# Two orders in the second attention: ScalarE's direct heads between two copies, and TensorE's next scores in front of the fourth turn

## The reference

```python
q = proj(query, w_q, b_q)          # 16 heads of 16 features
k = proj(key, w_k, b_k)
v = proj(value, w_v, b_v)
scores = jnp.einsum('bhqd,bhkd->bhqk', q, k) / np.sqrt(D_K)
attn = jax.nn.softmax(scores, axis=-1)
out = jnp.einsum('bhqk,bhkd->bhqd', attn, v)
out = out.transpose(0, 2, 1, 3).reshape(B, S, D_MODEL)
out = jnp.einsum('bsd,ed->bse', out, w_o) + b_o
```

## Time and profile before

| what | value |
|---|---|
| median of 3 runs | 601.71 us (600.31 to 602.09) |
| the profiled execution's own time | 600.69 us |
| its span | 599.0 us |
| TensorE's mean granted clock over the span | 0.953 |
| busy share of TensorE, VectorE, ScalarE, POOL over the span | 86%, 63%, 53%, 25% |
| second attention, from the first scores to the last turns | about 296 to 400 us |

### The profile page before, as it was taken

The page is one execution under the profiler, slowest core; times in us unless marked ns, Lnnn a source line. Parts: engine busy times, 40 slices in busy tenths (PEclk is TensorE's granted clock), DMA queues, the critical chain, the costliest instruction groups (busy, mean ns, idle before and its releaser), DMA issues.

```text
span 599.0 us, 9299 instructions
## 1 busy us (share of the span) xinstructions
PE 513.8 (86%) x3283; PEld 362.7 (61%) x3283; DVE 376.5 (63%) x937; ACT 317.3 (53%) x654; POOL 152.6 (25%) x218
## 2 busy tenths in 40 slices
PE   0869999899999700899989999996799999999994
PEld 0548866644444300787657687874667776777773
DVE  6765689945489989788688699987403432143101
ACT  1527658823389969781388899984222112211220
POOL 2716525000000000000323133111234354434531
PEclk9979999999999955999999999999699999999998
DMA  7900000000000000025000001015133536353410
GB/s 227 308 4 2 1 2 1 2 0 1 0 0 0 1 1 0 1 77 205 1 1 2 21 18 37 2 37 176 28 110 120 185 119 204 116 184 119 134 44 22
DMA packets 31994, 37.58 MB, mean 63 GB/s; under 512 B 8656, under 2 KB 27728, under 8 KB 31952
## 3 DMA queue, kind: packets, MB, share of 16 engines
q1 hardware_dynamic: 28880, 29.07, 15.0%
q0 software_dynamic: 3072, 7.95, 4.6%
HBM read 30.14 MB, written 6.88 MB: 62 GB/s over the span
## 4 chain that ended last, share of the span: by engine, by line
PE 68%; DVE 16%; ACT 10%; issue 2%; DMA 2%; SPq 1%; POOLq 0%; POOL 0%; DVEq 0%
PE pA L2043 12%; PE pB L2061 9%; PE pC L1712 6%; PE pC L1751 5%; PE pA L1745 3%; PE pB L1761 3%; ACT arena L609 3%; PE pA L1667 2%; PE pC L1575 2%; PE pC L1667 2%; PE pB L1667 2%; ACT XIT L706 2%; PE pC L2054 2%; DVE am L1168 2%; PE pB L1841 2%
## 5 line engine op out<-in xcount | busy, mean ns | idle before, releaser
L487 POOL TENSOR_TENSOR arena<-KT,par 128x256 f32<-128x256 f32 x32 | 18.9, 613 | 248.3 <-DVE XIT L1242 186.4
L2043 PE MATMUL pA<-arena 128*128 128x320 f32 x256 | 74.1, 438 | 0.4 <-ACT arena L882 0.4
L894 ACT ACTIVATE arena<-pA 128x320 f32<-128x320 f32 x64 | 28.0, 437 | 71.9 <-PE pA L2043 71.2
L2061 PE MATMUL pB<-arena 128*128 128x256 f32 x256 | 59.3, 385 | 0.0
L2043 PEld LDWEIGHTS pA<-arena 128*128 128x128 f32 x256 | 47.4, 190 | 18.9 <-issue 1.1
L2061 PEld LDWEIGHTS pB<-arena 128*128 128x128 f32 x256 | 47.4, 190 | 9.4 <-issue 3.1
L1134 DVE TENSOR_REDUCE am<-arena 128x1 f32<-128x512 f32 x48 | 32.1, 681 | 23.0 <-ACT arena L646 22.9
L1712 PE MATMUL pC<-wdnT,XIT 128*128 128x256 f32 x192 | 42.9, 381 | 1.8 <-DVE XIT L1242 1.8
L1318 DVE TENSOR_REDUCE rm<-pA 128x16 f32<-128x2048 f32 x16 | 36.7, 2291 | 8.7 <-PE pA L1745 8.7
L1712 PEld LDWEIGHTS pC<-wdnT,XIT 128*128 128x128 f32 x192 | 36.0, 190 | 7.9 <-DVE XIT L1242 2.8
L523 POOL DMA_INDIRECT out<-arena,token x24 | 23.5, 978 | 55.0 <-DVE arena L1466 43.9
(11 more groups left out here) (342 smaller groups left out, 1156.5 us busy)
## 6 DMA issues: line engine op xcount, KB each, us to landing
arena<-in_L_ffn_wi SPq DMA_DIRECT2D x8, 1024.0 KB, 5.4
arena<-in_L_ffn_wo SPq DMA_DIRECT2D x8, 1024.0 KB
X<-in_x SPq DMA_DIRECT2D x4, 512.0 KB, 5.7
arena<-in_ctx SPq DMA_DIRECT2D x4, 512.0 KB, 5.9
out<-X SPq DMA_DIRECT2D x4, 512.0 KB, 2.9
token_rows<-arena SPq DMA_DIRECT2D x4, 512.0 KB, 5.5
arena<-in_L_ffn_w_up SPq DMA_DIRECT2D x1, 768.0 KB, 9.1
arena<-in_L_ffn_w_gate SPq DMA_DIRECT2D x1, 768.0 KB, 10.2
```

What stands on the lines that cost most here:

```text
L894: nc.scalar.activation(HT[:, u, f, :], ps[2 + f % 2][:, 0:ROWS], ACT.Relu).then_inc(s["h_relu"], 1)
L2043: last = mm(ps[2 + f % 2][:, 0:ROWS], WI[:, u, k, f * P:(f + 1) * P], XET[:, u, k, :], start=(k == 0), stop=(k == KD - 1))
L2061: last = mm(ps[4 + c][:, 0:D], HT[:, u, f, c * P:(c + 1) * P], WO[:, u, f, :], start=(f == 0), stop=(f == NFT - 1))
```

## The change

On ScalarE, `direct(x)` moves in front of copy 2 of row y: it now stands between copies 1 and 2. On TensorE, `scores1(x+1)` moves in front of `turn_3(y)`. Nothing is added or removed, and no wait inside a step changes.

```diff
@@ ScalarE's loop
                     q_out(3, 1)
                 if 0 <= y < NB:
                     pt_copy(y, y % 2, 1)
+                if x < NB:
+                    direct(x, x % 2)
+                if 0 <= y < NB:
                     pt_copy(y, y % 2, 2)
                 if x < NB:
-                    direct(x, x % 2)
                     exps(x, x % 2, 0)
                 if 0 <= y < NB:
                     pt_copy(y, y % 2, 3)
@@ TensorE's loop
                     a_out(a, a % 2)
                 if 0 <= o < NB:
                     o_turn(o, o % 2)
+                if x + 1 < NB:
+                    scores1(x + 1, (x + 1) % 2)
                 if 0 <= y < NB:
                     turn_3(y, y % 2)
-                if x + 1 < NB:
-                    scores1(x + 1, (x + 1) % 2)
                 if x < NB:
                     turn_0(x, x % 2)
```

## The result

The changed kernel takes 606.25 us in the median of 7 runs (604.19 to 607.03), the kernel before 601.75 (600.31 to 604.5, 7 runs). The ratio is 1.0074 with a 95% interval of 1.0058 to 1.0089: slower by 4.5 us, which the interval leaves open between about 3.5 and 5.4. The forecast was 606.2 in a range of 603.4 to 608.4, slower with a chance of 0.89.

The account below looks back on a forecast made before the run. The kernel was taken as bound by a loop of waits through TensorE and ScalarE, 5.86 us a turn; 3.1 + 0.4 + 0.2 + 0.0 + 0.8 = +4.5 us on the median 601.71 gave 606.2, range 603.4 to 608.4.

Parts of the forecast that it names:

- What bounded the kernel: Second attention, ordinary turn: a loop of waits through TensorE and ScalarE, in which scores wait for `direct`, gives 5.87 us.
- Copy 2 behind `direct`: ScalarE, ordinary turn: the step from copy 1 to `direct` loses one copy, a gain of 0.48 us.
- Scores in front of `turn_3`: TensorE, ordinary turn: `turn_3` starts 1.08 us behind the scores; for TensorE a swap that costs nothing.
- The hold of copy 3: ScalarE: copy 3 waits for `turn_3`, idle 0.65 us; `at_copy` comes 0.79 later, net +0.31 a turn.
- S: The start of a turn's scores, from which the prediction counts the times of the other steps in us.
- The other turns: Second attention: ten ordinary turns +3.1 us, turn 1 +0.4, turn 3 +0.2, turn 4 0.
- the seven steps: ScalarE in turn 1: copy 3 and the list behind it before `direct(2)`, about 0.5 us each, 3.5 without a pause.
- The end: After the last turn: copy 2 now stands in front of `exps(15, 0)`, for which `last_turn(0)` waits; +0.8 us.
- The price of the Trainium skill: ScalarE: 0.73 us for each copy or exponential; the turn would grow about 0.5, the sum to about +7.
- The clock: Rival, TensorE: pauses lower the clock to 1.2 GHz; two such turns give some 616 us; chance 0.01.
- The gain that comes through: Rival, ordinary turns: scores follow `o_turn` at once, each turn falls by 0.16; -2.1 us, 599.6; chance 0.04.
- VectorE's second loop: Rival: VectorE's room of some 0.15 us a turn runs out, each turn costs 0.2 more; +7, 608.7; chance 0.08.

Follow-up runs that it names:

- run 2: ScalarE's half of the change alone, against the kernel before: TensorE's `turn_3` back in front of the scores; 607.45 us, ratio 1.0101.
- Run 1: The changed kernel with `exps(x, 1)` moved in front of copy 3 on ScalarE; 601.43 us, ratio 0.9999 to the kernel before.
- Run 6: The kernel before with, from turn 4, both changed orders, `exps(x, 1)` in front of copy 3 and copy 0 in front of `at_copy`; 600.53 us, ratio 0.9985.
- 3: The changed kernel plus one idle 128x256 copy in front of copy 3 on ScalarE; 605.78 us, ratio 1.0067 to the kernel before.
- run 4: The changed kernel plus one idle 128x256 copy behind copy 3 on ScalarE; 609.43 us, ratio 1.0127 to the kernel before.

## Why the prediction was right, step by step

- **What bounded the kernel.** The loop that I walked in the rows of before (scores, `turn_0`, `a_turn`, `at_copy`, copy 0, `turn_1`, copies 1 and 2, `direct`) was the right one. Six further kernels moved or loaded its steps, and every ordinary turn came out within 0.01 of what was expected (5.81 for 5.82, 6.36, 6.17, 6.47, 6.65 for 6.66, 5.80 for 5.79), the 6.36 with the reserve told at run 2.
- **Copy 2 behind `direct`: 0.48 gained.** Right: 355.37 to 355.86 is 0.49 from copy 1 to `direct`, where it was 0.97.
- **Scores in front of `turn_3`.** `turn_3` started 1.08 behind the scores, as `turn_0` had. Right. That this order costs TensorE nothing by itself is borne out by runs 1 and 6, which have it and turns of 5.81 and 5.80.
- **The hold of copy 3.** Predicted S + 1.78, measured 352.74 - 350.97 = 1.77. `exps` follows at 2.27 (2.26), `at_copy` at 2.78 (2.78), copy 0 at 3.05 (3.06), `turn_1` at 3.70 (3.70), copy 1 at 4.40 (4.40), `direct` at 4.89 (4.88), the next scores at 6.17 (6.17). I had announced an idle time of 0.65 in front of copy 3; the profile counts idle time from the end of the instruction before and says 0.48, from start to start it is 0.63. The 0.35 at `turn_1` is 0.30 in the row for the same reason.
- **The cause** is shown, not only argued: taking one exponential out of the held part removes the loss of an ordinary turn (1), and the same idle copy is free in front of the hold and costs in full behind it (3, 4).
- **The other turns.** Turn 1 and what follows to the scores of row 3: +0.53 for +0.4. The missing 0.1 is the one by which the scores of row 2 were to come sooner: they come 5.68 behind scores 1 as before, now held by VectorE's subtraction. From there the seven steps took the 3.5 of the prediction (copy 3 at 311.07, `direct` at 314.57). Turn 3: +0.21 for +0.2. Turn 4: -0.14 for 0; there `direct` ends at 338.15, early enough, and the scores at 338.63 follow `o_turn` (338.11) as soon as TensorE can. The ten ordinary turns: 9 x 0.304 + 0.30 = +3.03 for +3.1. The end: 7.51 against 6.72, +0.79 for +0.8. The sum is +4.4 for +4.5; the misses are small and partly cancel.
- **The end, read more closely.** The +0.8 there is all of the lateness of `at_copy` with nothing given back: behind the last scores TensorE waits for `exps(15, 0)`, and copy 2 stands in front of that in both orders. I had the size, but my reason, that copy 2 now stands in front of `exps(15, 0)`, is no difference between the kernels. Run 1 shows the same: its `at_copy` is 0.43 later than before, and its end takes 7.15, 0.43 more.
- **The price of the Trainium skill.** By "ScalarE: Activation LUTs", Rules for kernel authors, the turn would have grown by about 0.5 (1.25 later for `at_copy`, less 0.73 for copy 2). It grew by 0.304. Copy 3 took 0.50 of ScalarE's list (352.74 to 353.24) and the exponential 0.51 (353.24 to 353.75), where the page's figures give 0.73 for each. I had misapplied them: the page gives its 0.3 us for an activation whose bias is a `[128,1]` pointer operand, and the calls of the copies and of `exps` pass no bias. The four direct heads do pass one. For their 128 columns the figures give 0.41, an estimate, and the rows show 0.38 for each (the median of 64 before).
- **The clock.** TensorE stood still for 0.30 in front of `turn_1` in every turn. The ordinary turns are all 6.17 and eight matmuls of 128 columns take 1.09 as before. The profile's page grants nine tenths or more in all slices of this stage, the higher level of 2.4 GHz, as before; read for itself, the stretch from 303 to 406 us has a granted clock of 1.00. The rule of the Trainium skill, "TensorE: Matmul & The Clock Gate", A second HAM failure mode: psum-queue depth-cycling, did not show at pauses of this size, nor at 0.60 in run 4, whose turns are all alike too and whose granted clock is 1.00 from 338 to 400 us. One reading in the prediction was too narrow: the lower level was not granted around 210 to 240 us alone, slices 2 and 28 of the kernel before show 0.7 and 0.6, both outside the second attention.

```profile
PEclk9969999999999955999999999999699999999998
```

- **The rivals.** The gain that comes through needed `at_copy` by S + 2.43. Run 1 brings it to 2.42, and there the turn does fall below that of before, to 5.81: the point from which it decides was right. But it falls by 0.05 and not by 0.16, since `direct` stays the hold: it still stands behind copy 1, and copy 1 behind `turn_1`. Run 6, where copy 0 holds nothing any more, shows the whole of this shorter loop: `turn_1` 3.33 behind the scores, copy 1 another 0.70, `direct` 0.49, the next scores 1.29, together 5.81 for a turn of 5.80. I had overlooked that second link in the rival's price. VectorE's second loop did not close; 0.19 of its room is left, where I had walked about 0.15.

## What to carry to other kernels

When two engines with fixed lists feed each other, find the loop of waits and add it up from start to start; a step that is moved forward on it is worth what it gives only if nothing else in either list is pushed onto the loop. Moving work in front of a step delays whoever waits for that step, and everything that stands behind the waiting instruction in its own list: here the late copy 3 took 0.79 a turn, where moving copy 2 gave 0.48 back. A cheap test for where such a loop runs is an idle instruction put on either side of the suspected wait. Here, shorter than the wait, it was free on one side and cost its full slot on the other.

## What the runs showed that I had not expected

- Within each of the eight traces the nine ordinary turns agree to 0.01 us, while the start of scores 1, in front of which no kernel differs, moves by up to 1.8 us between the traces (302.8 to 304.6). Differences of this stage can be read far more finely from one trace than from the medians of many runs.
